# Layernorm statistics, tile transposes and router products of a pre-LN attention and MoE layer put in a new order

## What is computed

```python
def reference(x, Wq, bq, gate_w, w1, w3, w2, e_bias):   # x: 8 x 2048 x 1024
    # attention with Q = K = V
    q = layernorm(x) @ Wq + bq
    x = x + softmax(q @ q.T / 32) @ q
    # mixture of 32 experts, top 4, every expert computed for every token
    h = layernorm(x)
    scores = sigmoid(h @ gate_w.T)
    ids = top_k(scores + e_bias, 4)
    combine = scores at ids, divided by their sum, else 0        # 2048 x 32
    a = silu(h @ w1[e]) * (h @ w3[e])                            # 1024 -> 768
    return x + sum_e combine[:, e] * (a @ w2[e])
```

## Time and profile before

| | us |
|---|---|
| profiled execution | 4570.99 |
| its span, slowest of 8 cores | 4569.5 |
| spans of the 8 cores | 4552.2 to 4569.5 |
| two further runs | 4672.2 and 5470.74, median 5071.47 |
| PE busy in the span | 4420.6 (97%) |
| DVE, ACT, POOL busy | 1467.8, 589.3, 60.8 |

### The profile page before, as it was taken

How to read it: one execution, slowest core, us unless ns; L and a number is a source line. 1 busy time by engine, 2 the same in 40 slices (tenths; PEclk the granted TensorE clock), 3 DMA queues, 4 the chain that set the end, 5 groups by cost and what they waited for, 6 DMA issues and landing times.

```text
span 4569.5 us, 53922 instructions; the slowest of 8 cores (4552.2 to 4569.5 us)
## 1 busy us (share of the span) xinstructions
PE 4420.6 (97%) x20528; PEld 2039.4 (45%) x20528; DVE 1467.8 (32%) x2095; ACT 589.3 (13%) x942; POOL 60.8 (1%) x118
## 2 busy tenths in 40 slices
PE   4698899999999999999999999999999999999998
PEld 1244744444444444444444444444444444444443
DVE  2133433333333333333333333333333333333333
ACT  2320311111111111111111111111111111111110
POOL 0000000000000000000000000000000000000000
PEclk8899599999999999999999999999999999999999
DMA  3002202222222111222222222111222222222101
GB/s 97 1 1 34 50 1 42 42 42 42 42 42 42 28 23 34 42 42 42 42 42 42 42 42 42 31 23 30 42 42 42 42 42 42 42 42 42 34 9 74
DMA packets 17851, 173.81 MB, mean 38 GB/s; under 512 B 2112, under 2 KB 2368, under 8 KB 4544
## 3 DMA queue, kind: packets, MB, share of 16 engines
q0 software_dynamic: 16304, 153.10, 17.0%
q1 hardware_dynamic: 1296, 17.27, 1.0%
HBM read 315.07 MB, written 8.39 MB: 71 GB/s over the span
## 4 chain that ended last, share of the span: by engine, by line
PE 96%; ACT 2%; DVE 1%; issue 1%; DMA 0%; DVEq 0%; ACTq 0%
PE P L594 29%; PE P L555 29%; PE P L543 29%; PE P L328 2%; PE P L298 2%; PE P L258 2%; PE P L417 1%; PE P L391 0%; DMA T_x<-xp 0%; ACT T_A L249 0%; ACT T_B L272 0%; ACT T_fm L286 0%; ACT T_x2t L398 0%; PE P L264 0%; PE PTB L279 0%
## 5 line engine op out<-in xcount | busy, mean ns | idle before, releaser
L555 PE MATMUL P<-T_fm,T_A 128*128 128x512 bf16 x6144 | 1453.2, 379 | 7.1 <-DVE T_B L576 7.1
L543 PE MATMUL P<-T_fm,T_A 128*128 128x512 bf16 x6144 | 1453.1, 379 | 0.5 <-ACT T_lg L424 0.5
L576 DVE TENSOR_TENSOR T_B<-T_B,P 128x512 bf16<-128x512 bf16 x768 | 528.5, 688 | 2110.6 <-PE P L555 2110.4
L594 PE MATMUL P<-T_A,T_B 128*128 128x512 bf16 x4096 | 980.6, 379 | 2.1
L605 DVE SCALAR_TENSOR_TENSOR T_x<-P,T_c,T_x 128x512 f32<-128x512 f32 x1024 | 769.0, 751 | 569.7 <-PE P L594 569.7
L555 PEld LDWEIGHTS P<-T_fm,T_A 128*128 128x128 bf16 x6144 | 601.6, 98 | 733.7 <-issue 10.1
L543 PEld LDWEIGHTS P<-T_fm,T_A 128*128 128x128 bf16 x6144 | 601.5, 98 | 726.4 <-issue 2.7
L567 ACT ACTIVATE T_B<-P 128x512 bf16<-128x512 f32 x768 | 458.5, 597 | 3508.6 <-PE P L543 3508.6
L594 PEld LDWEIGHTS P<-T_A,T_B 128*128 128x128 bf16 x4096 | 394.6, 97 | 494.1 <-issue 188.7
L594 PE MATMUL P<-T_B 128*128 128x512 bf16 x2048 | 525.6, 379 | 0.0
L594 PEld LDWEIGHTS P<-T_B 128*128 128x128 bf16 x2048 | 200.4, 98 | 241.6
(11 more groups left out here) (62 smaller groups left out, 446.1 us busy)
## 6 DMA issues: line engine op xcount, KB each, us to landing
T_A<-w1d POOLq DMA_DIRECT2D x32, 1536.0 KB, 11.8
T_A<-w3d POOLq DMA_DIRECT2D x32, 1536.0 KB, 18.7
T_A<-w2d POOLq DMA_DIRECT2D x16, 1536.0 KB, 25.5
T_B<-w2d POOLq DMA_DIRECT2D x16, 1024.0 KB, 25.2
T_x<-xp SPq DMA_DIRECT2D x4, 2048.0 KB, 31.4
T_A<-w2d POOLq DMA_DIRECT2D x16, 512.0 KB, 20.9
T_A<-wq POOLq DMA_DIRECT2D x1, 2048.0 KB, 22.7
T_eb<-ebd SPq DMA_DIRECT2D x1, 256.0 KB, 39.7
```

Of the source, the lines that this page charges most:

```text
L543: ins = e.matmul(P0[:, gb * 512: gb * 512 + 512], w1_ap(par, hc, ic), T_fm[:, hc * (NT * 128) + c * 512: hc * (NT * 128) + c * 512 + 512], ...
L555: ins = e.matmul(P0[:, ub * 512: ub * 512 + 512], w3_ap(par, hc, ic), T_fm[:, hc * (NT * 128) + c * 512: hc * (NT * 128) + c * 512 + 512], ...
L576: v_a[(gc, ic)] = p.v(lambda e, gpar=gpar, ic=ic, ub=ub: e.tensor_tensor(at_ap(gpar, ic), s_ap(gpar, ic), P0[:, ub * 512: ub * 512 + 512], ...
L594: ins = e.matmul(out_slots[slot], at_ap(gpar, ic, (ts * 128, ts * 128 + 128)), w2_ap(par, ic, hh), start=(ic == 0), stop=(ic == NI - 1))
```

## The change

Three things are done, and nothing is computed otherwise.

- Stage 1: `emit_ln_group` of all four groups is emitted first. Then a loop over k emits the L242 transposes and L249 copy of tile k, the Q product and its cast of tile k-1, and the L279 transposes and L286 copy of tile k-2. `emit_ln_group` itself is split into `emit_ln_stats_group` (all up to L211) and `emit_ln_apply` (L215).
- Stage 3 and 4: the statistics of the second layernorm are emitted inside the attention loop, after every fourth tile's L337. Their outputs L215 come in one block of 16 after `srep_mm`.
- Stage 4: a loop over k emits on PE the L391 transposes of tile k, then L403 and L417 of tile k-1; on ACT the copy L398 of tile k, which now also waits for L417 of tile k-1, then L410 and L424 of tile k-1. All fixups are emitted after the loop.

The core of the diff (function bodies that are only moved are left out):

```diff
-        def emit_ln_group(g, x_of, lnf_of, xwaits_of):
+        def emit_ln_stats_group(g, x_of, xwaits_of):
...
+        def emit_ln_apply(j, x_ap, lnf_ap, extra=()):
+            return p.v(lambda e, j=j, o=lnf_ap, a=x_ap: e.tensor_scalar(
+                o, a, col(ST_RSTD + j), col(ST_NEGMUR + j), ALU.mult, ALU.add),
+                waits=list(extra))
+
+        def emit_ln_group(g, x_of, lnf_of, xwaits_of):
+            emit_ln_stats_group(g, x_of, xwaits_of)
+            return [emit_ln_apply(j, x_of(j), lnf_of(j))
+                    for j in range(4 * g, min(4 * g + 4, NT))]
...
+        for k in range(NT + 2):
+            if k < NT:
+                p1_tr_ln(k)
+            if 0 <= k - 1 < NT:
+                p1_q(k - 1)
+            if 0 <= k - 2 < NT:
+                p1_tr_q(k - 2)
...
+            if j % 4 == 3:
+                emit_ln_stats_group(
+                    j // 4,
+                    x_of=lambda jj: T_x[:, jj * H:(jj + 1) * H],
+                    xwaits_of=lambda jj: [("V", v_ev3[jj][1])])
 
         t_p3_all = p.cnt("T")
         v_p3_all = p.cnt("V")
...
+        for j in range(NT):
+            lnf2_toks[j] = emit_ln_apply(
+                j, T_x[:, j * H:(j + 1) * H], T_B[:, j * 1024:(j + 1) * 1024],
+                extra=([("T", t_p3_all), ("V", v_srep)] if j == 0 else []))
...
+            t_x2tr[j] = p.t(x2tr, waits=[("V", v_ev3[j][1]),
+                                         ("S", s_x2t[j - 1] if j else 0)])
...
+            t_tr4[j] = p.t(tr_ln2, waits=[("V", lnf2_toks[j]),
+                                          ("S", s_ev_ln2[j - 1] if j else 0)])
...
+            t_rt[j] = p.t(rtmm, waits=[("S", s_x2t[j]), ("dG", dG_all),
+                                       ("S", s_lgev[j - 1] if j else 0)])
+
+        for k in range(NT + 1):
+            if k < NT:
+                p4_x2tr(k)
+            if 0 <= k - 1 < NT:
+                p4_lnrt(k - 1)
+            if k < NT:
+                s_x2t[k] = p.s(lambda e, k=k: e.copy(T_x2t[:, :], P1[:, :]),
+                               waits=[("T", t_x2tr[k]),
+                                      ("T", t_rt[k - 1] if k else 0)])
+            if 0 <= k - 1 < NT:
+                jj = k - 1
+                s_ev_ln2[jj] = p.s(lambda e, j=jj: e.copy(
                     fmv(T_fm, j),
                     PTB[:, :].rearrange("p (c t) -> p c t", c=NH)),
...
+                s_lgev[jj] = p.s(lambda e, j=jj: e.copy(
                     T_lg[:, j * E:(j + 1) * E], P0[:, 0:E]),
...
+        emit_fixups(range(NT))
```

More of the change, by code:

```diff
@@ L238, in build_nc @@
                 lnf_toks[j] = toks[i]
[L239 to L289, removed]
@@ new lines, in p1_tr_ln, with tr_ln @@
+        def p1_tr_ln(j):
+            def tr_ln(e, j=j):
+                for k in range(NH):
+                    ins = e.transpose(
+                        PTB[:, k * 128:(k + 1) * 128],
+                        T_B[:, j * 1024 + k * 128: j * 1024 + k * 128 + 128],
+                        id_b[:, :])
+                return ins
+            t_tr1[j] = p.t(tr_ln, waits=[("V", lnf_toks[j]), ("dI", 32),
+                                         ("S", s_ev_ln1[j - 1] if j else 0)])
+            s_ev_ln1[j] = p.s(lambda e, j=j: e.copy(
+                fmv(T_A, j),
+                PTB[:, :].rearrange("p (c t) -> p c t", c=NH)),
+                waits=[("T", t_tr1[j])])
@@ new lines, in p1_q, with qmm @@
+        def p1_q(j):
+            def qmm(e, j=j):
+                base = (j % 2) * 1024
+                for half in range(2):
+                    for hc in range(NH):
+                        e.matmul(P0[:, base + half * 512: base + half * 512 + 512],
+                                 T_A[:, A_LN1T + hc * (NT * 128) + j * 128:
+                                     A_LN1T + hc * (NT * 128) + j * 128 + 128],
+                                 T_A[:, A_WQ + hc * H + half * 512:
+                                     A_WQ + hc * H + half * 512 + 512],
+                                 start=(hc == 0), stop=False)
+                    ins = e.matmul(P0[:, base + half * 512: base + half * 512 + 512],
+                                   ones_b[:, :],
+                                   bq_bf[:, half * 512: half * 512 + 512],
+                                   start=False, stop=True)
+                return ins
+            t_q[j] = p.t(qmm, waits=[("S", s_ev_ln1[j]), ("dW", dW_all),
+                                     ("V", v_ones_b),
+                                     ("S", s_ev_qtok[j - 2] if j >= 2 else 0)])
+            s_ev_qtok[j] = p.s(lambda e, j=j: e.copy(
+                T_B[:, j * 1024:(j + 1) * 1024],
+                P0[:, (j % 2) * 1024:(j % 2) * 1024 + 1024]),
+                waits=[("T", t_q[j])])
@@ new lines, in p1_tr_q, with tr_q @@
+        def p1_tr_q(j):
+            def tr_q(e, j=j):
+                for k in range(NH):
+                    ins = e.transpose(
+                        PTB2[:, k * 128:(k + 1) * 128],
+                        T_B[:, j * 1024 + k * 128: j * 1024 + k * 128 + 128],
+                        id_b[:, :])
+                return ins
+            t_tr2[j] = p.t(tr_q, waits=[("S", s_ev_qtok[j]),
+                                        ("S", s_ev_qt[j - 1] if j else 0)])
+            s_ev_qt[j] = p.s(lambda e, j=j: e.copy(
+                fmv(T_fm, j),
+                PTB2[:, :].rearrange("p (c t) -> p c t", c=NH)),
+                waits=[("T", t_tr2[j])])
@@ L377, in emit_fixups @@
                     ALU.mult, ALU.add))
[L379 to L410, removed]
@@ new lines, in build_nc, with p4_x2tr, x2tr @@
+        for j in range(NT):
+            lnf2_toks[j] = emit_ln_apply(
+                j, T_x[:, j * H:(j + 1) * H], T_B[:, j * 1024:(j + 1) * 1024],
+                extra=([("T", t_p3_all), ("V", v_srep)] if j == 0 else []))
+        def p4_x2tr(j):
+            def x2tr(e, j=j):
+                for k in range(NH):
+                    ins = e.transpose(
+                        P1[:, k * 128:(k + 1) * 128],
+                        T_x[:, j * H + k * 128: j * H + k * 128 + 128],
+                        id_f[:, :])
+                return ins
+            t_x2tr[j] = p.t(x2tr, waits=[("V", v_ev3[j][1]),
+                                         ("S", s_x2t[j - 1] if j else 0)])
@@ new lines, in p4_lnrt, with tr_ln2, rtmm @@
+        def p4_lnrt(j):
+            def tr_ln2(e, j=j):
+                for k in range(NH):
+                    ins = e.transpose(
+                        PTB[:, k * 128:(k + 1) * 128],
+                        T_B[:, j * 1024 + k * 128: j * 1024 + k * 128 + 128],
+                        id_b[:, :])
+                return ins
+            t_tr4[j] = p.t(tr_ln2, waits=[("V", lnf2_toks[j]),
+                                          ("S", s_ev_ln2[j - 1] if j else 0)])
+            def rtmm(e, j=j):
+                for hc in range(NH):
+                    ins = e.matmul(P0[:, 0:E],
+                                   T_x2t[:, hc * 128:(hc + 1) * 128],
+                                   T_gw[:, hc * E:(hc + 1) * E],
+                                   start=(hc == 0), stop=(hc == NH - 1))
+                return ins
+            t_rt[j] = p.t(rtmm, waits=[("S", s_x2t[j]), ("dG", dG_all),
+                                       ("S", s_lgev[j - 1] if j else 0)])
@@ L411, in build_nc @@
                     fmv(T_fm, j),
                     PTB[:, :].rearrange("p (c t) -> p c t", c=NH)),
[L413 to L421, removed]
@@ L422, in build_nc @@
-                t_rt[j] = p.t(rtmm, waits=[("S", s_x2t[j]), ("dG", dG_all),
-                                           ("S", s_lgev[j - 1] if j else 0)])
-                s_lgev[j] = p.s(lambda e, j=j: e.copy(
+                    waits=[("T", t_tr4[jj])])
+                s_lgev[jj] = p.s(lambda e, j=jj: e.copy(
                     T_lg[:, j * E:(j + 1) * E], P0[:, 0:E]),
-                    waits=[("T", t_rt[j])])
-            if g > 0:
-                emit_fixups(range(4 * (g - 1), 4 * g))
@@ L429, in build_nc @@
-        emit_fixups(range(4 * (NG - 1), NT))
+                    waits=[("T", t_rt[jj])])
+        emit_fixups(range(NT))
         macc = T_B[:, B_MACC:B_MACC + NE_COL]
```

## The result

The changed kernel is 0.78% faster: a ratio of 0.9922, with a 95% interval of 0.990 to 0.9943. That is a small gain, but the interval does not reach 1. Its profiled execution took 4529.06 us against 4570.99 before, and its span 4527.2 against 4569.5: the span is 42.3 us shorter. The forecast was 38.2 us less, 4532.8. The median over all 29 timed executions, however, is 4758.16 us (before: 4718.35 over 28), which lies outside the stated range of 4490 to 4635. In about half of the executions of either kernel the cores of one die or of both ran at a lower clock and the time was up to 920 us longer; the ratio leaves these out.

The account below looks back on a forecast made before the run. PE-bound score, attention and expert stages hold nothing to win; only stages 1 and 4 can change. Stage 1 gains 49.4 us, stage 4 loses 11.2: 38.2 less than 4570.99, so 4532.8 us, range 4490 to 4635.

Parts of the forecast that it names:

- the step from the sum to the measured time: From the profiled 4570.99 us, 38.2 less gives 4532.8; a run measured like the lower of two shown would give 4634.
- Stage 1, per tile: Pipelined loop of stage 1: a PE step of 5.18 us with no wait in the steady state.
- The rule that the upper clock does not engage for transposes: Rival, chance 0.03: transposes in stage 1 never at the upper level, 32 x 0.4 = 13 us more on PE, 4546.
- The rival that the clock stays mixed: Stage 1: most tiles keep one half at the lower level, 22 us more, 4555; chance 0.12.
- Stage 1, the start: Four square roots in ACT's queue stand before the first copy, which starts at about 69.0 instead of 31.63 us.
- the hold: First copy of stage 1 waiting behind all four layernorm square roots on ACT, at a cost of 37 us.
- Stage 1, the sum: Scores start at 158.9 instead of 208.29 us, so stage 1 gives 49.4 us.
- Stage 3: Second layernorm's statistics between attention evictions: 12.8 us of DVE per first block inside 13.8, so costed at nothing.
- The column sums: End of stage 3: srep_mm waits for the last group's statistics and starts at 441.6 instead of 431.65 us.
- Stage 4, per tile: Single T_x2t buffer makes copy and PE take turns: cycle 7.38 us against 6.60, stage 4 loses 11.2 us.
- the rival with 0.12: Stage 4 partly at the upper clock level: cycle 4.53 us there, seven tiles per core give 4514, all 4490; chance 0.12.

Follow-up runs that it names:

- e6_hoist_only: Kernel before with only the layernorms of all four groups emitted first, tiles in their old order; ratio 1.0053, quickest times 4599.6 and 4600.0 us.
- e3_no_hold: Changed kernel with each later group's layernorm emitted two tiles before its first transposes instead of all groups first; ratio 0.9825, quickest times 4490.4 to 4492.0 us.
- e4_x2t_two: Changed kernel with two buffers in turn for the transposed f32 tile T_x2t in stage 4; ratio 0.9792, quickest times 4475.4 to 4476.1 us.
- e8_filler: Changed kernel with 12 useless bf16 matmuls behind each router product, filling PE's wait for the T_x2t copy; ratio 0.9875, lowest time 4502.9 us.

## Why the prediction was right and where it failed

**What failed: the step from the sum to the measured time.** The prediction said of the two further runs of the kernel before: "A run measured like the lower one would give 4634, and the range keeps that end". It took the lower of them, 4672.2, less the gain, as the upper end, and gave no reason for leaving out the other, 5470.74. Neither was within 100 us of the profiled 4570.99, and they were the only sign of how far executions spread. The runs showed in its place that times far above 4634 are common: the 29 of the changed kernel go from 4527.7 to 5414.43 with a median of 4758.16, the 28 of the kernel before from 4566.33 to 5486.08 with a median of 4718.35. By these medians the changed kernel would be 40 us slower, so they do not measure the change. The cause of the spread was not looked for. What could be predicted from the trace was the ratio, and there 0.9916 was forecast and 0.9922 (0.990 to 0.9943) measured.

**Stage 1, per tile.** Right: 5.19 us for 5.18, no wait in the steady state, clock 0.99. The transposes ran at 0.61 us for 8 in each step, so the row was right. The rule that the upper clock does not engage for transposes (the Trainium skill, page "TensorE: Matmul & The Clock Gate", section "Part 4: PE-mode transpose") does not hold here. The rival that the clock stays mixed fell too.

**Stage 1, the start.** Right: the first copy at 69.64 for 69.0. `e6_hoist_only` and `e3_no_hold` show the hold from both sides, the scores 25 us later and the time 37 us shorter, and that ACT's list makes it.

**Stage 1, the sum.** Right: 159.47 for 158.9, 48.8 us gained for 49.4.

**Stage 3.** Costed at nothing, and DVE's blocks did stay covered: PE has no wait for L353. But the stages of scores and attention took 2.7 us more. All matmuls of the attention product are as fast as before (110.67 us); the scores L314 took 113.4 busy for 110.7, and the loss is at their start: the first 60 matmuls took 15.8 us, while the earlier trace rows have 36 in 7.9, which makes 13.1 for 60. This differs from core to core in either kernel: before, six cores had 112.4 and core 7 113.5, and in the changed kernel cores 5 and 6 had 110.7. Core 1 of before, from which the rows are, was a lucky one. This term was missing from the sum; it is a matter of the clock at the start of the scores, and nothing shows that the change made it.

**The column sums.** Right in place and size: idle 11.09 us, of which 1.19 were there before.

**Stage 4, per tile.** The mechanism was right, the cycle of 7.40 us and the 15 waits of 1.25 as worked out. The size was off: "stage 4 loses 11.2 us" measured 4.7. The mis-sized term is 14 x 7.38 = 103.3 us, which measured 96.7, because the clock came up in about every third tile. That was the rival with 0.12, and it came in on every core, with less than it was given (a mean cycle of 6.91, where seven tiles at the upper level would have made about 5.95). The old side of the difference was core 1 alone, at the lower level throughout. For the slowest core that was the right row; for six others, with 106.2 to 106.7 us before, the loss of stage 4 was 19 to 20 us and 11.2 was too little. That the total came within 4 us is in part luck: the clock of stage 4 gave 6.5 more than forecast, and the start of the scores took 2.7.

**What the sum did not price** is that the new wait of 1.25 us costs twice. The prediction named PE's idle time as a reason against the upper level in stage 4, but gave it no term: the wait counted 1.4 us per tile, and the clock was taken as low before and after. `e4_x2t_two` and `e8_filler` show that the clock hung on that wait.

## What to carry to other kernels

When work is hoisted out of a loop, look for the one small instruction of it that sits in another engine's queue: a square root of 0.21 us held PE for 37 us, and had only to be emitted two tiles later. When a pipeline interleaves two tiles, count the buffers between the stages first: with one buffer the copy and its reader take turns, whatever the order says. Where the granted clock is low and PE has short waits in each turn of a loop, a wait can be worth more than its length; and a count taken "of everything so far" as a wait value must be looked at again when something is put in front of it. And before the slowest core is taken as the old side of a difference, look at the other cores: here its stage 4 was some 15 us longer than that of six others.

## What the runs showed of the hardware

- With 1.25 us of idle PE in each 7.4 us, a loop of f32 products of 32 columns and transposes ran at a granted clock of 0.56, mostly at 1.2 GHz (window 405 to 485 of the changed kernel). With no wait in it the same instructions went to 2.4 GHz in the third tile and stayed, 5.98 to 3.12 us per tile (`e4_x2t_two`, core 1); with useless matmuls in the wait the clock of the same window was 0.88 (`e8_filler`).
- The same kernel on the same chip need not have the same clock on its cores: stage 4 of the kernel before had 0.53 and 122.0 us on core 1, and 0.63 and 106.2 us on core 3.
- Transposes of 128x128 bf16 run at the upper level when it is granted: 8 in 0.61 us, one each 0.06 us in steady state.
